# Flamingo block with routed experts on one core: biases loaded earlier, tile steps without a loop, table work cut in pieces, last gathers without a barrier

## The chip, the cores and the metric

One Trainium2 chip, one of its cores. The metric is the device time of one execution in microseconds (us). Four engines compute: PE (TensorE, matrix multiply, writes PSUM), DVE (VectorE), ACT (ScalarE) and POOL (GpSimd); SP (SyncE) only starts transfers. Each engine works through its own list of instructions and waits on semaphores for the others. PEld is the weight load of PE. A q behind an engine's name (DVEq, POOLq) is its sequencer, the part that reads the instructions, loads registers and waits.

## What is computed

```python
x = x + tanh(g_xattn) * attention(layernorm(x), ctx, ctx)     # 32 batches of 128 rows, width 512
z = layernorm(x)
logits = tanh(z @ Wg1.T) @ Wg2.T                              # 8 experts
top 2 experts of each row, weights = softmax of their two logits
up   = z @ Wup[e].T + bup[e]        # 512 -> 256
h    = silu(up)
down = h @ Wdown[e].T + bdown[e]    # 256 -> 512
x = x + tanh(g_ffn) * (weight1 * down1 + weight2 * down2)
```

All values are f32. The biases bup and bdown are the same for every row, so they are spread over all 128 partitions.

## The kernel before

**First phase.** A software pipeline of 39 steps does attention, norm and routing for 32 batches and scatters each normed row to two places in `slots`, one for each chosen expert. Batches 0 to 20 go to the first part, 21 to 31 to the second. At its end SP, PE, ACT and DVE meet at the semaphore `phase1_over`, and behind that SP loads the two biases (`bup` 1 MB, `bdn` 2 MB) and DVE, PE and ACT begin the tiles.

**Tiles.** The rows of `slots` are worked off in 78 tiles of 128 rows (49 of the first part, 29 of the second), each with one expert. In step s the engines work on several tiles at once: PE transposes the rows of tile s-1 (line 1096), transposes the activations of tile s-3 (L1103), multiplies tile s-2 by `Wup` (L1112 to 1114, 12 matmuls) and tile s-3 by `Wdown` (L1125 to 1127, 6 matmuls). Each f32 product is made of a high and a low part, so ACT copies the high part (`zh` L626, `hh` L621) and DVE makes the low part (`zl` L883, `hl` L877). DVE's order in a step is fixed by the code: read the expert's number from `tab_e` into a register (L295, a `TENSOR_LOAD` that its sequencer does), then `hl`, `zl`, `u_sb` (L892), `t_sb` (L896), `y_sb` (L905), then table work if the step has any, then the mixing of a batch. SP loads tile s and stores the result of tile s-4.

The steps 0 to 15 and 48 to 81 are written out; the steps 16 to 47 are a loop of two turns with 16 steps each (`tile_pipeline`).

**Tables.** `tables(part, n)` works out from the counts of each expert which expert and which rows a tile has (`tab_e`, `tab_r`) and where each row's result lies (`rows_all`). Each instruction reads what the one before wrote, so most go through `then`, which counts up `tab_step` and makes DVE wait for it. For the first part it runs in steps 30 to 34 of the first phase, and its last piece in tile step 5; the weights of the two choices (`coef`) follow in tile steps 6 and 7, and the second part's table in tile steps 8 to 12.

**Mixing.** From tile step 56 on, the 21 batches of the first part are finished beside the tiles: POOL gathers the two rows of each token from `expert_out` (L508), ACT and DVE scale, DVE and POOL add to `r_in`, SP stores. The 11 batches of the second part come after the last tile. Before that all five engines meet at `phase2_over`; then SP loads `r_late` (L400), POOL gathers (L527, 22 gathers), DVE adds twice for each batch and SP stores.

Of the kernel before, what the change touches and what calls it, by code (L numbers as in the profile page):

```python
# [23 lines left out]
P = 128  # L24
# [79 lines left out]
def block_kernel(nc, x_d, ctx_d, gx_d, gf_d, wg1_d, wg2_d, w_d, bup_d, bdn_d, out_d):  # L104
# [5 lines left out]
    with top:  # L110
# [41 lines left out]
        rows_f = sb("rows_f", [P, 2 * NA], F32, p12)  # L152
# [3 lines left out]

        z = [sb(f"z{i}", [P, D], F32, p1) for i in range(RING)]
        slot_i = [sb(f"slot_i{i}", [P, 2], I32, p1) for i in range(RING)]
# [5 lines left out]
        v_aug = [sb(f"v_aug{i}", [P, KV * 32], F32, p1) for i in range(RING)]  # L164
        q_t = [sb(f"q_t{i}", [P, D], F32, p1) for i in range(RING)]
        k_t = [sb(f"k_t{i}", [P, 2 * P], F32, p1) for i in range(RING)]
        probs = sb("probs", [P, KV * G * S], F32, p1)
# [39 lines left out]
        p23 = ExitStack()  # L207
        r_in = [sb(f"r_in{i}", [P, D], F32, p23) for i in range(RRING)]
# [7 lines left out]
        bup = sb("bup", [P, E * HE], F32, p2)  # L216
        bdn = sb("bdn", [P, E * D], F32, p2)             
# [53 lines left out]
        phase1_over, phase2_over = sem("phase1_over"), sem("phase2_over")  # L271
# [36 lines left out]
        def _(sp):  # L308
# [57 lines left out]
            def tile_step(s, u, fresh):  # L366
# [10 lines left out]
                if isinstance(s, int) and s >= 48 and s < 48 + RRING:  # L377
                    if s == 48:
                        sp.wait_ge(scatter_over, 1)
                    load_residual(s - 48)  # L380
# [784 lines left out]
```

## Time and profile before

| | |
|---|---|
| three timed runs | 813.27, 813.95, 819.04 us; median 813.95 |
| the profiled execution | 824.84 us, of which the span from first to last instruction is 823.1 |
| busy in the span | PE 689.5 us (84%), DVE 566.0 (69%), ACT 380.5 (46%), POOL 293.8 (36%) |
| mean granted TensorE clock | 0.946 of full speed |
| chain that ended last | PE 62%, DVE 15%, issue 8%, DMA 7%, POOL 4% |

A timeline row reads: start, length, engine, line, operation, output<-inputs, and in brackets how long the engine was idle before it and what ended that. "issue" is time in which an engine waited for nothing that the profile shows. Times count from the start of the span.

### The profile page before, as it was taken

The numbers are of one execution on the slowest core, as the hardware profiler recorded it, in microseconds if no ns is written. First come the engines' busy times: TensorE is split into PE (matmuls) and PEld (weight loads), VectorE is DVE, ScalarE is ACT, GpSimd is POOL, SyncE is SP. The second block draws the span as 40 slices with busy tenths as digits, with TensorE's granted clock in tenths as the row PEclk, the third lists the DMA queues.
The fourth block names the chain that finished last, engine by engine and source line by source line (L and its number), as shares of the span: only waits on it lengthen the run. The fifth ranks groups of instructions, "written<-read, shape, count | busy, mean of one in ns | idle before, by whom it ended". The sixth has DMA issues, their size and how long they took to land.

```text
span 823.1 us, 18197 instructions
## 1 busy us (share of the span) xinstructions
PE 689.5 (84%) x5232; PEld 465.5 (57%) x5233; DVE 566.0 (69%) x1543; ACT 380.5 (46%) x706; POOL 293.8 (36%) x406
## 2 busy tenths in 40 slices
PE   3788999999999999998897787999899978888700
PEld 2444554544444444454443676899789967767500
DVE  3567877877777777878863466777577757775625
ACT  2366766766666666666542232333233324433300
POOL 4123544545445454454333200000000026665465
PEclk9999999999999999999986699999999999999955
DMA  5532444434434344343222743444344659998778
GB/s 163 186 94 86 134 132 136 135 121 144 132 117 127 120 143 132 121 135 119 74 95 87 279 134 103 144 153 150 121 147 147 209 176 316 324 319 271 245 282 314
DMA packets 67845, 135.10 MB, mean 164 GB/s; under 512 B 8640, under 2 KB 12736, under 8 KB 67520
## 3 DMA queue, kind: packets, MB, share of 16 engines
q1 hardware_dynamic: 57088, 100.69, 38.1%
q0 software_dynamic: 10240, 33.56, 11.6%
q8 instruction: 33, 0.54, 0.3%
q14 instruction: 36, 0.29, 0.1%
q10 hardware_dynamic: 448, 0.02, 0.0%
HBM read 76.04 MB, written 58.20 MB: 163 GB/s over the span
## 4 chain that ended last, share of the span: by engine, by line
PE 62%; DVE 15%; issue 8%; DMA 7%; POOL 4%; SPq 2%; ACT 1%; DVEq 1%; another core or an unknown queue 1%; POOLq 0%; ACTq 0%
PE s_ps L979 11%; DVE nmax L762 9%; PE bank_a L958 7%; PE st_ps L1002 7%; PE bank_c L1019 3%; PE st_ps L1114 3%; PE st_ps L1112 3%; PE st_ps L1113 3%; PE s_ps L1096 3%; DMA z_s<-slots 3%; PE st_ps L1010 3%; POOL y_late L527 2%; PE bank_b L967 2%; DMA out<-r_in 2%; PE bank_c L1125 2%
## 5 line engine op out<-in xcount | busy, mean ns | idle before, releaser
L762 DVE TENSOR_REDUCE nmax<-s_ps 128x8 f32<-128x1024 f32 x128 | 156.4, 1222 | 91.0 <-PE s_ps L979 87.2
L979 PE MATMUL s_ps<-k_t,q_t 32*128 32x256 f32 x1024 | 153.8, 418 | 37.8 <-DVE nmax L762 35.8
L558 ACT ACTIVATE probs<-st_ps 128x1024 f32<-128x1024 f32 x128 | 131.1, 1024 | 115.5 <-PE st_ps L1010 113.0
L1002 PE MATMUL st_ps<-q_t,k_t 32*128 32x512 f32 x512 | 148.6, 656 | 1.2 <-ACT probs L558 1.0
L979 PEld LDWEIGHTS s_ps<-k_t,q_t 32*128 32x128 f32 x1024 | 91.9, 192 | 88.9 <-DVE nmax L762 49.2
L508 POOL DMA_INDIRECT y<-expert_out,rows_all x42 | 40.3, 960 | 205.9 <-DMA expert_out<-y_sb 196.3
L1112 PE MATMUL st_ps<-w_hi,zh 128*128 x312 | 96.5, 309 | 0.7 <-DVE zl L883 0.7
L1114 PE MATMUL st_ps<-w_hi,zl 128*128 x312 | 89.8, 288 | 0.0
L1113 PE MATMUL st_ps<-w_lo,zh 128*128 x312 | 89.3, 286 | 0.0
L631 ACT ACTIVATE t_sb<-u_sb 128x256 f32<-128x256 f32 x78 | 32.6, 417 | 109.7 <-DVE u_sb L892 105.3
L958 PE MATMUL bank_a<-probs,v_aug 128*32 128x512 f32 x512 | 70.8, 623 | 0.0
L485 POOL DMA_INDIRECT slots<-z,slot_i x64 | 64.4, 1006 | 16.4 <-issue 16.1
L1112 PEld LDWEIGHTS st_ps<-w_hi,zh 128*128 128x128 f32 x312 | 60.6, 194 | 1.1 <-issue 1.1
L1113 PEld LDWEIGHTS st_ps<-w_lo,zh 128*128 128x128 f32 x312 | 61.2, 196 | 0.0
L1096 PE MATMUL s_ps<-ident_f,z_s 128*128 128x128 f32 x312 | 49.2, 283 | 13.5 <-DMA z_s<-slots 11.8
L1114 PEld LDWEIGHTS st_ps<-w_hi,zl 128*128 128x128 f32 x312 | 60.3, 193 | 0.0
L896 DVE SCALAR_TENSOR_TENSOR t_sb<-t_sb,u_sb 128x256 f32<-128x256 f32 x78 | 33.2, 426 | 37.9 <-ACT t_sb L631 34.5
L883 DVE TENSOR_TENSOR zl<-s_ps,zh 128x512 fp32r<-128x512 f32 x78 | 53.7, 689 | 5.7 <-ACT zh L626 2.2
L1096 PEld LDWEIGHTS s_ps<-ident_f,z_s 128*128 128x128 f32 x312 | 38.8, 145 | 28.4 <-DMA z_s<-slots 16.2
L476 POOL TENSOR_TENSOR x_res<-x_res,z 128x512 f32<-128x512 f32 x32 | 40.5, 1267 | 30.3 <-DVE z L666 30.3
L1010 PE MATMUL st_ps<-nm_t,pick 32*128 32x512 bf16 x256 | 50.6, 382 | 0.0
L626 ACT ACTIVATE zh<-s_ps 128x512 fp32r<-128x512 f32 x78 | 46.3, 593 | 1.2 <-PE s_ps L1096 1.2
(153 smaller groups left out, 1423.7 us busy)
## 6 DMA issues: line engine op xcount, KB each, us to landing
z_s<-slots SPq DMA_DIRECT2D x78, 256.0 KB
expert_out<-y_sb SPq DMA_DIRECT2D x78, 256.0 KB
x_in<-in_x SPq DMA_DIRECT2D x32, 256.0 KB, 2.7
wst<-in_w SPq DMA_DIRECT2D x32, 256.0 KB, 2.6
x_res<-in_x SPq DMA_DIRECT2D x32, 256.0 KB
x_scratch<-x_res SPq DMA_DIRECT2D x32, 256.0 KB, 2.0
r_in<-x_scratch SPq DMA_DIRECT2D x21, 256.0 KB
out<-r_in SPq DMA_DIRECT2D x21, 256.0 KB
```

The lines of the kernel that those rows point to most:

```text
L485: g.indirect_dma_start(out=slots_d[int(split_at(b7))], out_offset=bass.IndirectOffsetOnAxis(ap=slot_i[q7][:, j:j + 1], axis=0), in_=z[q7][ ...
L558: a.activation(out, st_ps[:, :].rearrange("t (k n) -> t k n", k=2), ACT.Exp, scale=HD ** -0.5).then_inc(exp_done[half], 1)
L762: v.tensor_reduce(out, s_ps[:, :].rearrange("s (r g c t) -> s r g c t", r=2, g=2, c=2), X_AXIS, ALU.max, negate=True).then_inc(max_done, 1)
L883: v.tensor_tensor(zl[p][:, :], bank[p][:, :], zh[p][:, :].bitcast(F32), ALU.subtract).then_inc(zl_done, 1)
L958: last = t_.matmul(bank_a[32 * j:32 * j + 32, :], v_aug[r][:, 32 * k:32 * k + 32], probs[:, k * G * S:(k + 1) * G * S], start=True, stop=True,
L979: last = t_.matmul(s_ps[:, HALF * rr + 2 * P * gg:HALF * rr + 2 * P * (gg + 1)], q_t[r2][row:row + ROWS32, P * g_:P * (g_ + 1)], k_t[r2][r ...
L1002: t_.matmul(st_ps[:, HALF * rr:HALF * (rr + 1)], k_t[r][row:row + ROWS32, P * i:P * (i + 1)], q_t[r][row:row + ROWS32, :], start=True, sto ...
L1010: last = t_.matmul(st_ps[:, HALF * rr:HALF * (rr + 1)], pick[i][row:row + ROWS32, :], nm_t[p][row:row + ROWS32, :], start=False, stop=True ...
L1096: last = t_.transpose(bank[p][:, P * c:P * c + P], z_s[r][:, P * c:P * c + P], ident_f[:, :])
L1112: t_.matmul(o, zh[p][:, P * c:P * c + P], w_hi[:, cols], start=(c == 0), stop=False)
L1113: t_.matmul(o, zh[p][:, P * c:P * c + P], w_lo[:, cols], start=False, stop=False)
L1114: last = t_.matmul(o, zl[p][:, P * c:P * c + P], w_hi[:, cols], start=False, stop=(c == DC - 1))
```

## The change

Four things. (1) `bup` and `bdn` get memory that is free earlier, and SP loads them behind the loads of tiles 0 to 3 and ahead of `phase1_over`, after waits for the last readers of the memory. (2) `tile_pipeline` has no loop: all 82 steps are written out. The first four residual loads come in steps 40 to 43 instead of 48 to 51. (3) `tables` has 16 pieces instead of 5 (and one more for the first part): the first phase does three of them in each of steps 30 to 34, piece 15 of the first part is in tile step 6, the weights are in steps 8 to 11 (one instruction each), and the second part's pieces are in steps 14 to 29, one in each step. (4) `phase2_over` is gone: SP waits for the last matmul (`dn_done`) before it loads `r_late`, POOL for the last matmul and the last two stores of results (`y_stored`) before it gathers, DVE for its data.

```diff
 def tile_pipeline(eng, step):
-    first, last, unroll = 16, 48, 16
-    for s in range(first):
-        step(s, s % unroll, s == 0)
-    with eng.Fori(0, (last - first) // unroll) as i:
-        for u in range(unroll):
-            step(i * unroll + (first + u), u, u == 0)
-    for s in range(last, TILES + 4):
-        step(s, s % unroll, s == last)
+    for s in range(TILES + 4):
+        step(s, s % 16, s == 0)
...
             for t in range(RING):
                 load_tile(t, t)
+            sp.wait_ge(w_lo_done, B)
+            sp.wait_ge(n_done, B)
+            sp.wait_ge(kt_done, B)
+            sp.wait_ge(v_done, B)
+            sp.wait_ge(qt_done, B)
+            sp.wait_ge(st_done[1], 2 * B)
+            sp.wait_ge(pv_done, 2 * B)
+            sp.dma_start(bup[:, :], bup_d.to_broadcast([P, E * HE])).then_inc(bup_loaded, 16)
+            sp.dma_start(bdn[:, :], bdn_d.to_broadcast([P, E * D])).then_inc(bdn_loaded, 16)
             for p in range(2):
                 sp.wait_ge(res_stored[p], ring2(B - 2 + p, p))
             sp.drain().then_inc(phase1_over, 1)
             sp.wait_ge(phase1_over, 4)
-            sp.dma_start(bup[:, :], bup_d.to_broadcast([P, E * HE])).then_inc(bup_loaded, 16)
-            sp.dma_start(bdn[:, :], bdn_d.to_broadcast([P, E * D])).then_inc(bdn_loaded, 16)
...
             tile_pipeline(sp, tile_step)
-            for p in range(2):
-                last = TILES - 1 - (TILES - 1 - p) % 2
-                sp.wait_ge(y_stored[p], ring2(last, p))
-            sp.drain().then_inc(phase2_over, 1)
-            sp.wait_ge(phase2_over, 5)
+            sp.wait_ge(dn_done, TILES)
...
-            pool.drain().then_inc(phase2_over, 1)
-            pool.wait_ge(phase2_over, 5)
             pool.wait_ge(rows_done, 2)
+            pool.wait_ge(dn_done, TILES)
+            for p in range(2):
+                last = TILES - 1 - (TILES - 1 - p) % 2
+                pool.wait_ge(y_stored[p], ring2(last, p))
...
-                if isinstance(s, int) and 5 <= s < 8:
-                    tables(0, s)
-                if isinstance(s, int) and 8 <= s < 13:
-                    tables(1, s - 8)
+                if s == 6:
+                    tables(0, 15)
+                if 8 <= s < 12:
+                    weights_of_choices(s - 8)
+                if 14 <= s < 30:
+                    tables(1, s - 14)
```

On DVE, the first table step of the tiles (step 8 before): all instructions of `tables(1, 0)` stand between `y_sb` and the register load of the next step.

```order
L905 SCALAR_TENSOR_TENSOR y_sb<-bank_c,bdn 128x512
L692 TENSOR_TENSOR count<-run,ebase 128x8 [waits run_done]
L694 TENSOR_SCALAR upto<-e_diff 128x64 [waits tab_step]
L695 SCALAR_TENSOR_TENSOR past<-count,iota_t 128x88
L698 TENSOR_REDUCE ntile<-past 128x8 [waits tab_step]
L295 TENSOR_LOAD tab_e [waits tab_step]
L295 ISA x2
L877 TENSOR_TENSOR hl<-bank_q,hh 128x256 [waits dn_done,hh_done]
```

The same engine after the change, steps 14 and 15, which hold the first two of the sixteen pieces.

```order
L914 SCALAR_TENSOR_TENSOR y_sb<-bank_c,bdn 128x512
L693 TENSOR_TENSOR count<-run,ebase 128x8 [waits run_done]
L694 TENSOR_SCALAR upto<-e_diff 128x64
L288 TENSOR_LOAD tab_e [waits tab_step]
L288 ISA x2
L886 TENSOR_TENSOR hl<-bank_q,hh 128x256 [waits dn_done,hh_done]
L892 TENSOR_TENSOR zl<-s_ps,zh 128x512 [waits up_done,zh_done]
L901 ISA [waits tanh_done,up_done]
L901 TENSOR_TENSOR u_sb<-st_ps,bup 128x256
L905 SCALAR_TENSOR_TENSOR t_sb<-t_sb,u_sb 128x256 [waits ht_done,tanh_done]
L914 ISA [waits y_stored0,dn_done]
L914 SCALAR_TENSOR_TENSOR y_sb<-bank_b,bdn 128x512
```

The pieces are shorter, and the wait for `tab_step` still stands on the register load, now in each step that has a piece ending in `then`: 14 of the 16 table pieces and 3 of the 4 pieces of the weights.

On SP, the end of the tiles before:

```order
L376 DMA expert_out<-y_sb 128x512 [waits y_done]
L390 DMA out<-r_in 128x512 [waits mix2]
L400 DMA r_late<-x_scratch 128x512 [waits y_stored1,y_stored0,phase2_over]
L400 DMA r_late<-x_scratch 128x512 x10
L390 DMA out<-r_in 128x512 [waits mix2]
```

And after:

```order
L376 DMA expert_out<-y_sb 128x512 [waits y_done]
L390 DMA out<-r_in 128x512 [waits mix2]
L396 DMA r_late<-x_scratch 128x512 [waits dn_done]
L396 DMA r_late<-x_scratch 128x512 x10
L390 DMA out<-r_in 128x512 [waits mix2]
```

The places in the list are the same; the loads of `r_late` wait for the last matmul alone. On POOL the last gathers (L527) trade `phase2_over`, which stood behind POOL's own drain, for `dn_done` and `y_stored`.

## Rows read from the trace of the kernel before

**Rows 1.** Windows: start:end and length, busy time of PE, PEld, DVE, ACT, POOL, PE's clock, DMA.
```profile
586.00:655.80 69.80, 69.72 (x475) 62.73 (x474) 51.54 (x101) 25.39 (x59) 0.00 (x0) 1.00 0.52 164
655.80:780.00 124.20, 105.35 (x651) 88.50 (x649) 81.48 (x156) 47.78 (x102) 66.14 (x62) 0.97 0.84 277
784.00:786.40 2.40, 0.00 (x0) 0.00 (x0) 0.00 (x0) 0.00 (x0) 0.00 (x0) 0.50 0.00 0
```

**Rows 2.** Timeline of DVE, a step without table work.
```profile
516.95 0.69 DVE L905 SCALAR_TENSOR_TENSOR y_sb<-bank_c,bdn 128x512 f32<-128x512 f32 x1
517.91 0.42 DVE L877 TENSOR_TENSOR hl<-bank_q,hh 128x256 fp32r<-128x256 f32 x1 [0.27 <-ACT hh L621]
...
520.44 0.69 DVE L905 SCALAR_TENSOR_TENSOR y_sb<-bank_b,bdn 128x512 f32<-128x512 f32 x1
```

**Rows 3.** Timeline of DVE, tile steps 5 to 8 and the end of step 12.
```profile
476.48 0.69 DVE L905 SCALAR_TENSOR_TENSOR y_sb<-bank_b,bdn 128x512 f32<-128x512 f32 x1
...
477.44 0.42 DVE L877 TENSOR_TENSOR hl<-bank_a,hh 128x256 fp32r<-128x256 f32 x1 [0.18 <-ACT hh L621]
...
479.97 0.69 DVE L905 SCALAR_TENSOR_TENSOR y_sb<-bank_c,bdn 128x512 f32<-128x512 f32 x1
...
480.79 0.35 DVE L740 RECIPROCAL coef<-coef 128x32 f32<-128x32 f32 x1
481.88 0.42 DVE L877 TENSOR_TENSOR hl<-bank_q,hh 128x256 fp32r<-128x256 f32 x1 [0.74 <-DVE coef L740]
...
484.37 0.69 DVE L905 SCALAR_TENSOR_TENSOR y_sb<-bank_b,bdn 128x512 f32<-128x512 f32 x1 [0.23 <-PE bank_b L1127]
484.98 0.23 DVE L743 TENSOR_SCALAR coef<-coef,gates 128x32 f32<-128x32 f32 x1
...
485.96 0.42 DVE L877 TENSOR_TENSOR hl<-bank_a,hh 128x256 fp32r<-128x256 f32 x1 [0.52 <-issue]
...
488.43 0.69 DVE L905 SCALAR_TENSOR_TENSOR y_sb<-bank_c,bdn 128x512 f32<-128x512 f32 x1 [0.21 <-PE bank_c L1127]
...
490.88 0.42 DVE L877 TENSOR_TENSOR hl<-bank_q,hh 128x256 fp32r<-128x256 f32 x1 [1.01 <-DVE ntile L698]
...
513.46 0.69 DVE L905 SCALAR_TENSOR_TENSOR y_sb<-bank_b,bdn 128x512 f32<-128x512 f32 x1 [0.22 <-PE bank_b L1127]
```

**Rows 4.** Windows: sum over the five stretches that hold the second part's table work.
```profile
sum 5.44, PE 5.44 PEld 5.22 DVE 4.95 ACT 4.12 POOL 0.00; mean PE 1.09 PEld 1.04 DVE 0.99 ACT 0.82 POOL 0.00
```

**Rows 5.** Line 295: duration in ns min/median/max of DVE's register loads.
```profile
L295 DVEq TENSOR_LOAD <-tab_e x81: 298/305/673, 458.5 to 772.5; - x81
```

**Rows 6.** Timeline of DVE around the loop's begin and its second turn.
```profile
518.40 0.69 DVE L883 TENSOR_TENSOR zl<-s_ps,zh 128x512 fp32r<-128x512 f32 x1
...
533.16 0.69 DVE L883 TENSOR_TENSOR zl<-s_ps,zh 128x512 fp32r<-128x512 f32 x1
...
571.91 0.69 DVE L883 TENSOR_TENSOR zl<-s_ps,zh 128x512 fp32r<-128x512 f32 x1
...
581.81 0.42 DVE L877 TENSOR_TENSOR hl<-bank_a,hh 128x256 fp32r<-128x256 f32 x1 [3.56 <-issue]
...
593.79 0.69 DVE L883 TENSOR_TENSOR zl<-s_ps,zh 128x512 fp32r<-128x512 f32 x1
```

**Rows 7.** Timeline: SP's load of tile 3, and the first use of the bias.
```profile
451.87 0.34 SPq L349 DMA_DIRECT2D z_s<-slots  x1
...
461.78 0.41 PE L1114 MATMUL st_ps<-w_hi,zl 128*128 x1
...
462.77 0.42 DVE L892 TENSOR_TENSOR u_sb<-st_ps,bup 128x256 f32<-128x256 f32 x1 [2.69 <-DMA bup<-in_bup]
```

**Rows 8.** Chain that ended last (start, length, what), on POOL's queue behind its last addition.
```profile
782.87 3.59 issue
```

**Rows 9.** Waits of SP's queue from 775 to 790: us in total, times, longest.
```profile
SPq L396 <- DMA expert_out<-y_sb: 1.2, 1, 1.2
```

**Rows 10.** Timeline, the first late gather.
```profile
787.19 0.96 POOL L527 DMA_INDIRECT y_late<-expert_out,rows_all  x1 [4.32 <-POOLq L522]
```

More of the change, by code:

```diff
@@ L151, in block_kernel @@
         shift = sb("shift", [P, 2 * NA], F32, p12)
-        rows_f = sb("rows_f", [P, 2 * NA], F32, p12)
         p1 = ExitStack()
-        z = [sb(f"z{i}", [P, D], F32, p1) for i in range(RING)]
-        slot_i = [sb(f"slot_i{i}", [P, 2], I32, p1) for i in range(RING)]
         wst = sb("wst", [P, WCHUNK], F32, p1)
@@ L163, in block_kernel @@
         q_perm = sb("q_perm", [P, D], F32, p1)
-        v_aug = [sb(f"v_aug{i}", [P, KV * 32], F32, p1) for i in range(RING)]
         q_t = [sb(f"q_t{i}", [P, D], F32, p1) for i in range(RING)]
         k_t = [sb(f"k_t{i}", [P, 2 * P], F32, p1) for i in range(RING)]
+        v_aug = [sb(f"v_aug{i}", [P, KV * 32], F32, p1) for i in range(RING)]
+        z = [sb(f"z{i}", [P, D], F32, p1) for i in range(RING)]
+        slot_i = [sb(f"slot_i{i}", [P, 2], I32, p1) for i in range(RING)]
         probs = sb("probs", [P, KV * G * S], F32, p1)
@@ L207, in block_kernel @@
         p23 = ExitStack()
+        bup = sb("bup", [P, E * HE], F32, p23)
+        bdn = sb("bdn", [P, E * D], F32, p23)
         r_in = [sb(f"r_in{i}", [P, D], F32, p23) for i in range(RRING)]
@@ L215, in block_kernel @@
         p2 = ExitStack()
-        bup = sb("bup", [P, E * HE], F32, p2)
-        bdn = sb("bdn", [P, E * D], F32, p2)
         zh = [sb(f"zh{i}", [P, D], F32R, p2) for i in range(2)]
@@ L270, in block_kernel @@
         scattered = [sem(f"scattered{i}") for i in range(RING)]
-        phase1_over, phase2_over = sem("phase1_over"), sem("phase2_over")
+        phase1_over = sem("phase1_over")
         bup_loaded, bdn_loaded, scatter_over = sem("bup_loaded"), sem("bdn_loaded"), sem("scatter_over")
@@ L376, in tile_step @@
                     sp.dma_start(y_d[part][bass.ds((t - TILE0[part]) * P, P), :], y_sb[p][:, :]).then_inc(y_stored[p], 16)
-                if isinstance(s, int) and s >= 48 and s < 48 + RRING:
-                    if s == 48:
+                if isinstance(s, int) and s >= 40 and s < 40 + RRING:
+                    if s == 40:
                         sp.wait_ge(scatter_over, 1)
-                    load_residual(s - 48)
+                    load_residual(s - 40)
                 for m in mixed_at(s - 2 if isinstance(s, int) else s):
@@ L639, in _ @@
             tile_pipeline(act, tile_step)
-            act.drain().then_inc(phase2_over, 1)
         @block.vector
@@ L687, in tables @@
                 nt, t0 = NTILES[part], TILE0[part]
+                cols = slice(2 * first, 2 * (first + nb))
+                ov = past[:, 0:E * nb].rearrange("p (e i) -> p e i", e=E)
+                un = upton[:, :].rearrange("p (e i) -> p e i", e=E)
                 pv_ = past[:, 0:nt * E].rearrange("p (t e) -> p t e", e=E)
                 pw_ = pastw[:, 0:nt * E].rearrange("p (t e) -> p t e", e=E)
+                bv = pastw[:, 0:2 * nb * E].rearrange("p (n e) -> p n e", e=E)
                 if n == 0:
                     dve.wait_ge(run_done, first + nb)
-                    then(v.tensor_tensor(count[:, :], run[part][:, :], ebase[part][:, :], ALU.subtract))
-                    ov = past[:, 0:E * nb].rearrange("p (e i) -> p e i", e=E)
-                    step_of(v.tensor_scalar(upto[:, :], e_diff[:, :], 0.0, None, ALU.is_le))
+                    step_of(v.tensor_tensor(count[:, :], run[part][:, :], ebase[part][:, :], ALU.subtract))
+                    then(v.tensor_scalar(upto[:, :], e_diff[:, :], 0.0, None, ALU.is_le))
+                if n == 1:
                     then(v.scalar_tensor_tensor(ov, count[:, :].unsqueeze(2).to_broadcast([P, E, nb]), 1.0 / P,
@@ L697, in tables @@
                                                 ALU.mult, ALU.is_gt))
+                if n == 2:
                     then(v.tensor_reduce(ntile[:, :], ov, X_AXIS, ALU.add))
-                if n == 1:
-                    un = upton[:, :].rearrange("p (e i) -> p e i", e=E)
+                if n == 3:
                     step_of(v.memset(drop[:, E:E + 1], 0.0))
@@ L854, in step @@
                                     ALU.is_equal).then_inc(masks_done, 1)
-                if isinstance(s, int) and s >= TAB0 and s - TAB0 < 5:
-                    tables(0, s - TAB0)
+                if isinstance(s, int) and s >= TAB0:
+                    for n in range(3 * (s - TAB0), min(3 * (s - TAB0) + 3, 15)):
+                        tables(0, n)
             pipeline(dve, step, STEPS, LOOP0, NA + O_SLOT, RING)
@@ L919, in _ @@
             tile_pipeline(dve, tile_step)
-            dve.drain().then_inc(phase2_over, 1)
-            dve.wait_ge(phase2_over, 5)
             for i in range(NB):
@@ L1130, in _ @@
             tile_pipeline(pe, tile_step)
-            pe.drain().then_inc(phase2_over, 1)
 _INS = ["x", "ctx_512", "g_xattn", "g_ffn", "wg1", "wg2", "w", "bup", "bdn"]
```

35 lines of the change are left out of this document (20 added, 15 removed).

## The prediction

> **What bounds the kernel now.** I read the windows by stage first [rows 1]. From 586 to 655.8 us, tiles without any mixing, PE is busy 69.72 of 69.80 us: PE is the bound, and a step takes 3.50 us. From 655.8 to 780, beside the mixing, the DMA engines are busy 0.84 of the time and move 277 GB/s, and the 124 us are bought by transfers as much as by PE. From 784 to 786.4 no engine and no transfer does anything. So the reader should see three things to ask of each edit: does it stand in a PE-bound step, in the DMA-bound stretch (nothing here does), or in a pause.
>
> Then I read DVE's timeline step by step. In a step without table work `y_sb` starts at 516.95, `hl` at 517.91 and the next `y_sb` at 520.44 [rows 2]: 0.96 us and then 2.53 us, 3.49 together. The 2.53 us are a chain that leaves DVE and comes back: `hl`, the six matmuls with `Wdown`, `y_sb`. Where DVE is late this chain shrinks only to 2.47 us (485.96 to 488.43) [rows 3]. So a step stays at 3.50 us only while `hl` starts at most 3.50 - 2.47 = 1.03 us behind the start of `y_sb`, and each us beyond is paid in full. Though DVE is busy 69% of the span, what is put behind `y_sb` has only 1.03 - 0.96 = 0.07 us of cover. The 0.96 us hold one more thing: DVE's sequencer reads the expert's number during `y_sb`. A `then` in front of that read forbids it.
>
> **Part 3, the table in pieces.** Before, steps 6 to 12 hold this work. From 479.97 to 513.46 seven steps take 33.49 us [rows 3]; seven free ones take 24.5, so it costs 9.0 us.
>
> What does one piece cost? In step 7 one instruction with a wait behind it stands in the way (L743; L744 has no wait). `hl` starts 485.96 - 484.37 = 1.59 us behind `y_sb`, 0.56 too late. The instruction itself holds 0.25 of that, so 0.31 is fixed. In step 6 the two instructions run from about 480.58 to 481.14 (0.56), `hl` is at 481.88, 1.91 behind `y_sb` and 0.88 too late: fixed 0.32. In step 8 four instructions take 0.88 (one of the five stretches of [rows 4]), `hl` is at 490.88, 2.45 behind, 1.42 too late: fixed 0.54 [rows 3]. The fixed part is the register load with what follows it, which now starts only when the table instruction has ended. It took DVE 298 ns at the least, 305 in the median and 673 at the most [rows 5]. In step 5, where the one instruction has no wait, `hl` is 477.44 - 476.48 = 0.96 behind `y_sb`: free.
>
> After the change 14 table pieces and 3 of the weights end in a wait; the others are free like step 5. Their instructions: 5.44 us for the second part's [rows 4], less 0.52 for those at the ends of steps 11 and 12 that have no wait, so 4.9, and 0.56 + 0.25 for the weights: 5.7 together. With 17 times 0.32 it is 5.7 + 5.4 = 11.1 us. With 17 times 0.54 it is 14.9. Against 9.0 before, this edit loses **2.1 us** (up to 5.9). I take 0.32, since the short pieces come as early behind `y_sb` as those of steps 6 and 7 did. Cutting makes nothing cheaper: the sum of the instructions stays, and the fixed part is paid 17 times instead of 7. In the first phase the same instructions stay in the same steps 30 to 34, three pieces in each; nothing.
>
> The Trainium skill (DMA: Bandwidth & Descriptors, section Latency and other measured facts) gives a register load a floor of about 600 ns. The trace's median of 305 ns lies under it [rows 5]; by that floor each piece would cost 0.3 us more than I take, some 5 us in all, which is my second rival's case.
>
> **Part 2, no loop.** Loop turns cost time at two places. At the entry four steps from 518.40 to 533.16 take 14.76 us instead of 14.0: 0.8. At the second turn DVE starts `hl` at 581.81 after 3.56 us of "issue", and the five steps from 571.91 to 593.79 take 21.88 us instead of 17.5: 4.4 [rows 6]. "Issue" with all inputs there means that the sequencer has no instruction. Written out, both go: **5.2 us**. The steps that were written out before had no such stall, so I take nothing for the 32 new ones; they cost 0 to 2 us if the fetch is sometimes late. The residual loads eight steps earlier are four transfers in SP's queue in a stretch where the DMA engines are half idle (0.52) [rows 1]: nothing.
>
> **Part 1, biases early.** The first `u_sb` waits for `bup` until 462.77, while the last of its matmuls ends at 461.78 + 0.41 = 462.19 [rows 7]. SP issued the load of tile 3 at 451.87 [rows 7] and would issue `bup` right behind it instead of behind the barrier. `bup` then lands earlier by the same time, and half a us of it is enough: `u_sb` goes with the matmul, **0.5 us** (0 to 1). The seven new waits are on batches' work done before SP's last four tile loads; behind them in SP's list stand only its drain and `phase1_over`, for which DVE is the last. The 3 MB meet the last scatters, for which nobody waits until step 40. If SP's drain should hold until the biases have landed, the barrier opens late; I count that into the last rival.
>
> **Part 4, no barrier.** POOL's last addition ends at 782.87, then 3.59 us pass on POOL's queue in its drain, and only then the barrier opens [rows 8]; the last stores of results had landed at about 782.9, since SP waited 1.2 us for them behind its issue that ended at 781.7 [rows 9]. The first gather starts at 787.19 [rows 10]. Without drain and barrier it starts about 0.1 to 0.7 us behind 782.9, so 3.6 to 4.2 us earlier. What is late next is POOL's own issue of 22 gathers, 1.26 us each, which sets the tail before and after. The `r_late` loads start at 781.7 in the pause instead of together with the gathers, which can only relieve them. I take **3.8 us** (3 to 5).
>
> **Sum.** 0.5 + 5.2 + 3.8 - 2.1 = 7.4 us less. The profiled execution goes from 824.84 to 817.4. It was 10.9 us longer than the median of the three runs; I take the difference over unscaled: 813.95 - 7.4 = **806.5 us**.
>
> **Rivals.**
>
> *The pieces are dearer.* The fixed part is 0.54 for each, as in step 8. For it: steps 8 to 10 have it three times. Against: steps 6 and 7 have 0.32, and the new pieces are like those. Then 7.4 - 3.8 = 3.6 less: 810.3 us.
>
> *The pieces hide.* If the wait on `tab_step` costs nothing and the register load keeps its place under `y_sb`, a piece of 0.2 to 0.4 us fits into the gap in front of `hl` (0.27 us [rows 2]). Then the table costs about nothing instead of 9.0: 5.2 + 0.5 + 3.8 + 9.0 = 18.5 less, 795.5 us. For it: step 5 was free, and DVE is idle 31% of the time. Against: step 7, where one short instruction with a wait cost 0.56. The Trainium skill (VectorE: DVE Perf Modes, section The DRAIN you can't avoid) says that a semaphore behind each of a chain of DVE operations costs nothing extra; by that rule it would come out this way. The trace speaks against it where a register load, not another DVE operation, stands behind the wait.
>
> *The pause at the end stays.* The 3.6 us on POOL are not the drain but something the first late gather has to wait for in any case. For it: no row names what the drain waits for. Against: POOL's addition had ended, the stores had landed, and no transfer was under way [rows 1, 8, 9]. Then 7.4 - 3.8: 810.3 us, as the first.
>
> *Written-out steps starve.* Each of the 32 new step bodies is fetched for the first time, as the loop's first turn was, and two of the engines' lists grow. If a step lacks instructions for 0.24 us on the mean (7.4 / 32 = 0.23), the gain is gone; at 0.4 us it is 5 us slower, 819 us. For it: after a turn of the loop the sequencers stay behind for two more steps. Against: the steps written out before run at 3.50.
>
> **Chances.** My forecast 0.50; dearer pieces 0.18; hidden pieces 0.12; the pause stays 0.12; slower through fetch (or the drain on SP) 0.08. A measurement of this kernel tells about 1%, 8.1 us, from no change. Of my own case four in ten lie beyond that bound, 0.20, with the hidden pieces 0.32: faster 0.33, within 1% 0.60, slower 0.07. The range: the ends of the terms in my case are 0 + 3.5 + 3 - 5.9 = 0.6 and 1 + 5.2 + 5 - 2.1 = 9.1 less; the low end goes a little further towards the hidden pieces: 801.5 to 812.5.
>
> **What would show it.** In tile steps 14 to 29 of the new trace `hl` should start 1.5 to 1.9 us behind `y_sb` and a step should take 3.9 to 4.3 us, save in the steps of pieces 11 and 15. There should be no wait of 3 us for "issue" around tile 31. The first `u_sb` should wait for a matmul. The first late gather should start within a us of the last landed store, and the windows should show no stretch without transfers there. I am wrong if the register load slips under `y_sb` in spite of the wait, if the stall of the loop turns up elsewhere, or if the DMA-bound stretch of 124 us, which I leave as it is, comes out shorter or longer by some us.

## The result, and the profile after

The changed kernel takes 807.0 us in the median of 20 runs (802.6 to 817.9); before, on the same chip, takes 817.97 (20 runs). The ratio is 0.987, 95% interval 0.984 to 0.989: 10.7 us less (8.7 to 12.8). The forecast was 7.4 us less, 806.5 us. The profiled execution took 817.92 us, span 816.2, against 824.84 and 823.1 of before, so the two that can be compared row by row lie 6.9 us apart. Some executions are over 1.5% slower at a lower granted clock, the profiled ones of the changed kernel and of experiment 4 among them; the ratios here and below leave these out, the medians don't.

First the table step, on DVE's timeline of the changed kernel: the end of step 13, then the first two pieces, and far behind them a step without table work.

```profile
503.71 0.69 DVE L914 SCALAR_TENSOR_TENSOR y_sb<-bank_b,bdn 128x512 f32<-128x512 f32 x1
504.68 0.42 DVE L886 TENSOR_TENSOR hl<-bank_a,hh 128x256 fp32r<-128x256 f32 x1 [0.27 <-ACT hh L619]
...
507.17 0.69 DVE L914 SCALAR_TENSOR_TENSOR y_sb<-bank_c,bdn 128x512 f32<-128x512 f32 x1
...
507.85 0.18 DVE L694 TENSOR_SCALAR upto<-e_diff 128x64 f32<-128x64 f32 x1
508.78 0.42 DVE L886 TENSOR_TENSOR hl<-bank_q,hh 128x256 fp32r<-128x256 f32 x1 [0.74 <-ACT hh L619]
...
511.26 0.69 DVE L914 SCALAR_TENSOR_TENSOR y_sb<-bank_b,bdn 128x512 f32<-128x512 f32 x1 [0.22 <-PE bank_b L1136]
512.84 0.42 DVE L886 TENSOR_TENSOR hl<-bank_a,hh 128x256 fp32r<-128x256 f32 x1 [0.74 <-ACT hh L619]
...
515.32 0.69 DVE L914 SCALAR_TENSOR_TENSOR y_sb<-bank_c,bdn 128x512 f32<-128x512 f32 x1 [0.22 <-PE bank_c L1136]
...
589.41 0.69 DVE L914 SCALAR_TENSOR_TENSOR y_sb<-bank_b,bdn 128x512 f32<-128x512 f32 x1
590.37 0.42 DVE L886 TENSOR_TENSOR hl<-bank_a,hh 128x256 fp32r<-128x256 f32 x1 [0.27 <-ACT hh L619]
592.86 0.69 DVE L914 SCALAR_TENSOR_TENSOR y_sb<-bank_c,bdn 128x512 f32<-128x512 f32 x1
```

`hl` starts 1.61 and 1.58 us behind `y_sb` where a piece stands, 0.96 or 0.97 where none does; the steps take 4.09 and 4.06 us against 3.45. From `hl` to the next `y_sb` it takes 2.48 or 2.49 us with a piece and without; before had 2.47 and 2.53 [rows 2, 3]. The releaser named for a late `hl` is ACT's `hh`, but `hh` ended 0.93 us behind the start of `y_sb` in every one of these steps. Behind the piece, which ends at 508.03, DVE's sequencer runs the register load from 508.07 to 508.37 and what belongs to it until 508.66; in the free step ahead the load had started at 503.74, under `y_sb`. Experiments 1 and 2 test this reading. Without table work a step takes 3.45 or 3.46 us, not the 3.50 of before [rows 2]: nothing in the prediction has this.

The register load itself, by source line, in ns (minimum, median, maximum), answers to [rows 5]:

```profile
L288 DVEq TENSOR_LOAD <-tab_e x78: 299/304/1112, 456.7 to 769.1; - x78
```

The end of the tiles, on the timeline (POOL, SP and DVE), answers to [rows 8 to 10]:

```profile
776.40 0.69 DVE L914 SCALAR_TENSOR_TENSOR y_sb<-bank_c,bdn 128x512 f32<-128x512 f32 x1 [2.04 <-PE bank_c L1136]
777.12 0.32 SPq L376 DMA_DIRECT2D expert_out<-y_sb  x1
...
777.83 1.26 POOL L516 TENSOR_TENSOR r_in<-r_in,y 128x512 f32<-128x512 f32 x1 [2.45 <-DVE r_in L927]
...
779.99 0.96 POOL L525 DMA_INDIRECT y_late<-expert_out,rows_all  x1 [0.90 <-DMA expert_out<-y_sb]
```

The first late gather now waits for the landed store and nothing else. It starts 3.59 us behind the start of the last `y_sb` (7.01 us before, 780.18 to 787.19 [rows 10]).

Where the time went is read best between starts of `zl`, one for each tile. The n-th `zl` marks tile n-1. All numbers are us from DVE's timeline, and the last column runs to the end of the span.

| kernel | 2nd zl at | 2nd to 4th | 4th to 53rd | 53rd to 56th | 56th to 78th | 78th to end |
|---|---|---|---|---|---|---|
| before | 459.38 | 11.57 | 186.26 | 17.04 | 95.93 | 52.92 |
| after | 457.60 | 11.13 | 181.28 | 17.67 | 99.13 | 49.39 |
| difference | -1.78 | -0.44 | -4.98 | +0.63 | +3.20 | -3.53 |

The column from the 4th to the 53rd holds the loop, the table and the free steps; the last holds the barrier; the second holds the biases. The stretch from the 53rd to the 78th, in which the change has no term of the sum, is 3.8 us longer in this one execution; PE's mean granted clock in its two columns is 0.81 and 0.95 where before has 0.90 and 0.98.

### The profile page after: what moved, and what is told of

Its sections match the earlier page's. It is cut to its first block, busy times and chain, and to the rows that moved or that the text cites. A ratio compares the mean times of both kernels' runs of the same rounds, so it can differ in the third digit from the quotient of the medians.

```text
span 816.2 us, 17880 instructions
## 1 busy us (share of the span) xinstructions
PE 688.8 (84%) x5232; PEld 466.9 (57%) x5232; DVE 562.0 (69%) x1541; ACT 380.4 (47%) x706; POOL 293.8 (36%) x406
## 4 chain that ended last, share of the span: by engine, by line
PE 63%; DVE 15%; DMA 7%; issue 6%; POOL 3%; SPq 2%; DVEq 1%; ACT 1%; another core or an unknown queue 1%; PEld 0%; POOLq 0%; PEldq 0%
PE s_ps L988 12%; DVE nmax L770 9%; PE bank_a L967 8%; PE st_ps L1011 7%; DMA z_s<-slots 3%; PE bank_c L1028 3%; PE st_ps L1123 3%; PE bank_b L976 3%; PE st_ps L1121 3%; PE st_ps L1122 3%; DMA out<-r_in 3%; POOL y_late L525 3%; PE s_ps L1105 2%; PE st_ps L1019 2%; PE bank_c L1134 2%
```

## The experiments

All ratios below are against before on the same chip, with 95% intervals, and "the changed kernel" is the kernel of the result above. The first eight kernels ran on one chip, where before has a median of 808.2 to 808.3 us, the next two on a second (before 807.96), the last two on a third (before 819.22). The same table for all twelve comes behind them.

**1. The wait for a piece moved to the front of the next piece.** The changed kernel; a piece's last instruction counts up `tab_step` as before, but DVE waits for it only where the next piece begins, one tile step later.

```diff
+            def settle():
+                if link[0]:
+                    dve.wait_ge(tab_step, link[0])
...
+                last = then if part == 0 else step_of
+                if part == 1:
+                    settle()
...
                 if n == 2:
-                    then(v.tensor_reduce(ntile[:, :], ov, X_AXIS, ALU.add))
+                    last(v.tensor_reduce(ntile[:, :], ov, X_AXIS, ALU.add))
```

> The changed kernel, but a piece of the second part's table or of the weights no longer waits for its own end: the wait for tab_step stands in front of the next piece's instruction, one step later. If the price of a piece is the register load that starts only behind the wait, hl starts 0.96 to 1.1 us behind y_sb (1.5 to 1.8 in the changed kernel) in all of these steps except the one with two dependent instructions, the 11.4 us that the pieces cost shrink to 0.5 to 1.5, and the kernel is 10 us faster than the changed one, some 797 us where that has 807. If the instructions themselves or the semaphore cost the time, the steps stay at 3.9 to 4.3 us and nothing changes.

Measured: 783.87 us, ratio 0.968 (0.964 to 0.973). DVE's timeline of this kernel, two steps with one instruction each and then the piece with two dependent ones:

```profile
500.76 0.69 DVE L924 SCALAR_TENSOR_TENSOR y_sb<-bank_b,bdn 128x512 f32<-128x512 f32 x1
501.37 0.24 DVE L705 SCALAR_TENSOR_TENSOR past<-count,iota_t 128x88 f32<-128x88 f32 x1
501.73 0.42 DVE L896 TENSOR_TENSOR hl<-bank_a,hh 128x256 fp32r<-128x256 f32 x1
504.21 0.69 DVE L924 SCALAR_TENSOR_TENSOR y_sb<-bank_c,bdn 128x512 f32<-128x512 f32 x1
504.82 0.23 DVE L709 TENSOR_REDUCE ntile<-past 128x8 f32<-128x88 f32 x1
505.17 0.42 DVE L896 TENSOR_TENSOR hl<-bank_q,hh 128x256 fp32r<-128x256 f32 x1
...
511.31 0.69 DVE L924 SCALAR_TENSOR_TENSOR y_sb<-bank_c,bdn 128x512 f32<-128x512 f32 x1 [0.20 <-PE bank_c L1146]
512.87 0.42 DVE L896 TENSOR_TENSOR hl<-bank_q,hh 128x256 fp32r<-128x256 f32 x1 [0.55 <-issue]
```

The same instructions at the same places, and `hl` is 0.97 and 0.96 us behind `y_sb` instead of 1.58. An instruction of 0.24 us fits under the 0.27 us that DVE is idle there anyway [rows 2]. Only the piece with a wait left inside it is late (1.56). From the 8th to the 30th `zl` this kernel takes 76.91 us where the changed one takes 87.47: with 22 free steps of 3.455 (76.0) the table costs 0.9 us here and 11.5 there. So it is the wait's place that costs; experiment 2 tells the wait from the load behind it.

**2. The register load moved ahead of the piece, the wait left where it was.**

```diff
+                if 8 <= s < 11 or 14 <= s < 30:
+                    ahead.append(expert_of(dve, s - 1))
                 if s == 6:
                     tables(0, 15)
...
-                    expert[0] = expert_of(dve, s - 2)
+                    expert[0] = ahead.pop() if ahead else expert_of(dve, s - 2)
```

> The changed kernel, with the same waits behind each piece, but the expert's number of the next step is read into its register in front of the piece instead of behind it. If it is the order of wait and register load that costs, hl starts about 1.0 us behind y_sb for short pieces and 1.1 to 1.3 for those of 0.4 us and more, and 9 to 10 us of the 11.4 go. If a wait of DVE for its own instruction costs 0.3 us by itself, wherever the load stands, at most 2 us go.

Measured: 792.61 us, ratio 0.982 (0.976 to 0.988). DVE's timeline at the piece of one instruction that the changed kernel has at 511.87, after its `y_sb` of 511.26:

```profile
495.31 0.69 DVE L914 SCALAR_TENSOR_TENSOR y_sb<-bank_b,bdn 128x512 f32<-128x512 f32 x1
495.96 0.25 DVE L696 SCALAR_TENSOR_TENSOR past<-count,iota_t 128x88 f32<-128x88 f32 x1
496.32 0.42 DVE L886 TENSOR_TENSOR hl<-bank_a,hh 128x256 fp32r<-128x256 f32 x1
```

The stretch from the 8th to the 30th `zl` is 77.89 us, so the table costs 1.9; `hl` is 1.01 to 1.18 us behind `y_sb` in most pieces, though DVE waits behind each piece as in the changed kernel. The wait itself is nearly free: what cost 0.32 us was that the load could not start before it. Two different edits, which both let the load go ahead of the wait, take 10.6 and 9.6 us off this stretch; with that the price of a piece is shown. The medians of the two lie 8.7 us apart, which the steps do not explain; the four runs of experiment 2 spread from 785.8 to 796.5 us.

**3. The changed kernel with the old table.** `tables`, its calls and `rows_f` as in before, the rest as after.

```diff
-                if s == 6:
-                    tables(0, 15)
-                if 8 <= s < 12:
-                    weights_of_choices(s - 8)
-                if 14 <= s < 30:
-                    tables(1, s - 14)
+                if 5 <= s < 8:
+                    tables(0, s)
+                if 8 <= s < 13:
+                    tables(1, s - 8)
```

> The changed kernel with the table and the weights in the pieces and steps of the kernel before (steps 5 to 12, seven steps with waits). By the sum of the prediction the stretch costs 9.0 us instead of 11.4, so this is 2 to 2.5 us faster than the changed kernel, too little for the times but to be read from the steps. If cutting had helped, it would be slower than the changed kernel.

Measured: 798.18 us, ratio 0.988 (0.983 to 0.993). The table costs 8.9 us (from the 6th to the 14th `zl` 36.93 us, less eight steps of 3.50), against 11.5 in sixteen pieces. But from the 4th to the 53rd `zl` it takes 180.52 us and not 2.6 less than the changed kernel's 181.28, since its free steps take 3.50 us again. The two prices are each counted from the kernel's own free step (3.455 and 3.50), so their difference is not what the cut costs; experiments 3 and 5 together give that, below. That raised the question of experiments 5 and 6.

**4. POOL's drain put back alone** in front of the last gathers, with no meeting of the engines.

```diff
+            pool.drain().then_inc(pool_quiet, 1)
+            pool.wait_ge(pool_quiet, 1)
             pool.wait_ge(rows_done, 2)
```

> The changed kernel, and POOL drains its pipe once behind its last addition, with no barrier and no other engine in it. If the 3.6 us in front of the last gathers were POOL's own drain, the first late gather again starts 7 us behind the last y_sb instead of 3.6, and the kernel is 3.4 us longer than the changed one. If they were the meeting of five engines, the drain costs under 0.5 us and nothing changes.

Measured: 800.9 us, ratio 0.991 (0.987 to 0.994). POOL's and DVE's timeline at the end of the tiles:

```profile
766.54 0.69 DVE L916 SCALAR_TENSOR_TENSOR y_sb<-bank_c,bdn 128x512 f32<-128x512 f32 x1 [3.47 <-PE bank_c L1138]
...
767.97 1.26 POOL L516 TENSOR_TENSOR r_in<-r_in,y 128x512 f32<-128x512 f32 x1 [3.89 <-DVE r_in L929]
773.65 0.96 POOL L527 DMA_INDIRECT y_late<-expert_out,rows_all  x1 [4.42 <-POOLq L518]
```

7.11 us from `y_sb` to the gather, as before had 7.01, though only POOL waits here, and only for itself. The drain on POOL's queue (duration in ns, start in us):

```profile
L518 POOLq DRAIN  x1: 4807/4807/4807, 767.9 to 767.9; - x1
```

It begins with POOL's last addition and ends 3.51 us behind the end of it. The trace of before has a drain of the same 4807 ns. POOL's own drain is the pause; what the drain waits for no run shows.

**5 and 6. The addresses.** One is the changed kernel with an unused tensor of 168 bytes per partition where `rows_f` was; the other is before without `rows_f`, its values kept in `shift`.

```diff
 (changed kernel)
         shift = sb("shift", [P, 2 * NA], F32, p12)
+        pad = sb("pad", [P, 2 * NA], F32, p12)
 (before)
-        rows_f = sb("rows_f", [P, 2 * NA], F32, p12)
...
-    step_of(v.tensor_tensor(rows_f[:, cols], slot_all[:, cols], shift[:, 0:2 * nb], ALU.subtract))
+    step_of(v.tensor_tensor(shift[:, cols], slot_all[:, cols], shift[:, 0:2 * nb], ALU.subtract))
...
-    v.tensor_copy(rows_all[:, 0:2 * NA], rows_f[:, 0:2 * NA]).then_inc(rows_done, 1)
+    v.tensor_copy(rows_all[:, 0:2 * NA], shift[:, 0:2 * NA]).then_inc(rows_done, 1)
```

> This is the changed kernel with one more tensor that nothing uses: 168 bytes per partition at the place in memory where before had rows_f, so that every tensor behind it gets the address that it had before, apart from the biases. Theory A (addresses): the removed rows_f moved all later tensors by 168 bytes, and that is why a tile step without table work takes 3.46 us in the changed kernel and in three experiments, and 3.50 in before and in the experiment with the old table. Then the step is 3.50 here again, and the time between the zl of tile steps 2 and 53 is about 2.2 us longer than in the changed kernel (183.5 for 181.3). Theory B (instructions): the step is shorter because DVE's instructions or their order differ; then it stays at 3.46 and the stretch at 181.3.

> The kernel before without rows_f: the first part's rows are worked out in the tensor shift, in place, so that all later tensors lie 168 bytes lower; nothing else differs. Theory A (addresses): a tile step without table work goes from 3.50 to 3.46 us, and 49 of them give 2.2 us, of a time of some 808 (ratio about 0.997). Theory B (instructions): the step stays at 3.50, ratio 1.000.

Measured: 801.94 us (ratio 0.988, 0.971 to 1.004) and 808.78 us (1.001, 0.996 to 1.006): the medians can't show two us. The steps can. First DVE's timeline of the changed kernel with the unused tensor, three starts of `y_sb`:

```profile
601.13 0.69 DVE L915 SCALAR_TENSOR_TENSOR y_sb<-bank_c,bdn 128x512 f32<-128x512 f32 x1
604.62 0.69 DVE L915 SCALAR_TENSOR_TENSOR y_sb<-bank_b,bdn 128x512 f32<-128x512 f32 x1
608.11 0.69 DVE L915 SCALAR_TENSOR_TENSOR y_sb<-bank_c,bdn 128x512 f32<-128x512 f32 x1
```

3.49 us a step, while the same instructions without the tensor take 3.45 or 3.46. In before without `rows_f` (experiment 6) the steps between the 36th and the 39th `zl` take 3.46, 3.46 and 3.45 us where before has 3.50. PE's groups of both kernels between 585 and 640 us (line, tiles, count, busy us, mean ns of one); the changed kernel with the tensor, then without, the latter from 585.1:

```profile
L1122 PE MATMUL st_ps<-w_hi,zh 128*128 x63 | 19.1, 303 | 0.0
L1124 PE MATMUL st_ps<-w_hi,zl 128*128 x62 | 17.5, 283 | 0.0
L1123 PE MATMUL st_ps<-w_lo,zh 128*128 x62 | 17.4, 280 | 0.0
```

```profile
L1121 PE MATMUL st_ps<-w_hi,zh 128*128 x64 | 19.3, 301 | 0.0
L1122 PE MATMUL st_ps<-w_lo,zh 128*128 x64 | 17.9, 280 | 0.0
L1123 PE MATMUL st_ps<-w_hi,zl 128*128 x64 | 17.9, 279 | 0.0
```

The matmuls of `w_hi` with `zl` take 283 ns instead of 279 and those of `w_hi` with `zh` 303 instead of 301; those of `w_lo` take 280 in both. Theory A holds in both directions, but its price was wrong: 1.4 us from the 4th to the 53rd `zl` (182.26 against 180.8 to 180.9 in four kernels without the tensor; 186.26 against 184.78), not 2.2. I had counted all 49 steps, and in a step with table work DVE, not PE, sets the length (4.09 us in the first piece at either address).

Experiments 5 and 3 have the old addresses both, and differ in the table: 182.26 us from the 4th to the 53rd `zl` with sixteen pieces, 180.52 with the old five. The cut costs 1.7 us.

**7. Before with the tile steps written out** and nothing else (the first hunk of the diff).

> The kernel before with the tile steps written out and nothing else. My sum gave this 5.2 us: 0.8 at the loop's begin and 4.4 at its second turn; the ratio would be 0.9936, the steps at both places 3.50 like their neighbours, and no other step longer. A rival: the written-out steps starve an engine elsewhere, and single steps between 16 and 53 show stalls of 0.3 us or more that sum to more than 1 us; the ratio is then above 0.996.

Measured: 800.49 us, ratio 0.993 (0.988 to 0.998). From the 4th to the 53rd `zl` 180.64 us, 5.6 less than before. DVE's timeline where before had its 3.56 us of "issue" [rows 6]:

```profile
572.73 0.69 DVE L877 TENSOR_TENSOR zl<-s_ps,zh 128x512 fp32r<-128x512 f32 x1
576.24 0.69 DVE L877 TENSOR_TENSOR zl<-s_ps,zh 128x512 fp32r<-128x512 f32 x1
579.81 0.69 DVE L877 TENSOR_TENSOR zl<-s_ps,zh 128x512 fp32r<-128x512 f32 x1
583.31 0.69 DVE L877 TENSOR_TENSOR zl<-s_ps,zh 128x512 fp32r<-128x512 f32 x1
```

3.51, 3.57 and 3.50 us; no step between the 14th and the 53rd `zl` takes more than 3.58. Nothing starves.

**8. The changed kernel with the biases loaded behind `phase1_over`,** in their new memory.

```diff
-            sp.wait_ge(w_lo_done, B)
...
-            sp.wait_ge(pv_done, 2 * B)
-            sp.dma_start(bup[:, :], bup_d.to_broadcast([P, E * HE])).then_inc(bup_loaded, 16)
-            sp.dma_start(bdn[:, :], bdn_d.to_broadcast([P, E * D])).then_inc(bdn_loaded, 16)
             for p in range(2):
                 sp.wait_ge(res_stored[p], ring2(B - 2 + p, p))
             sp.drain().then_inc(phase1_over, 1)
             sp.wait_ge(phase1_over, 4)
+            sp.dma_start(bup[:, :], bup_d.to_broadcast([P, E * HE])).then_inc(bup_loaded, 16)
+            sp.dma_start(bdn[:, :], bdn_d.to_broadcast([P, E * D])).then_inc(bdn_loaded, 16)
```

> The changed kernel with the loads of both biases back behind phase1_over, their memory as in the changed kernel. My sum gave the early loads 0.5 us: the first u_sb waits for the bias again, 2.7 us idle on DVE ahead of it for under 2 without, and from the second to the fourth zl it is 11.6 us instead of 11.1; ratio to the changed kernel 1.0006, which its time can't show. A rival by which the early loads are worth 1.8 us or more: the end of the first phase is later as well, since SP issued the biases in front of its waits for the stores; then the first tile step starts 1 us or more later than in the changed kernel, beyond what it varies between runs.

Measured: 798.05 us, ratio 0.989 (0.978 to 0.999). The second `zl` starts at 451.30 us, within the 443.7 to 452.5 of the other experiments, so there is no sign of the rival; a spread of 9 us would hide its 1.8, though. The first `u_sb` goes with its matmul (2.34 us idle on DVE, released by PE), and the first `y_sb` waits 1.01 us for `bdn`; 9.76 us pass from the 2nd to the 4th `zl`, 0.3 to 0.5 more than in the four kernels that have 9.26 to 9.42 with early loads. The size was right and the place was not: here it is `bdn` that is late, and not `bup`.

**9. The best version.** Experiment 1, and the piece with two dependent instructions split.

```diff
                 if n == 4:
-                    then(v.tensor_reduce(tend[:, :], un, X_AXIS, ALU.add))
+                    last(v.tensor_reduce(tend[:, :], un, X_AXIS, ALU.add))
+                if n == 4.5 or (part == 0 and n == 4):
                     last(v.scalar_tensor_tensor(row0[:, :], tend[:, :], float(-P), run[part][:, :], ALU.mult, ALU.add))
...
-                if 14 <= s < 30:
-                    tables(1, s - 14)
+                if 14 <= s < 31:
+                    tables(1, s - 14 if s < 19 else 4.5 if s == 19 else s - 15)
```

> The changed kernel with the wait for a piece's result moved to the front of the next piece, one tile step later, and the one piece whose second instruction reads the first split in two, so the table has 17 pieces in steps 14 to 30. If the price of a piece is the wait ahead of the register load, no step holds more than about 0.1 us over its neighbours: the experiment with the wait moved alone had 0.9 us over in the table stretch, 0.57 of it in the piece that is now split, so about 0.4 stays, and the time is 0.3 to 0.6 us under that experiment's, which this measurement can't tell; against before some 0.97. A rival: each further piece has a fixed price of its own whatever it waits for, and the stretch is not shorter than before the split.

Measured: 789.58 us, ratio 0.969 (0.964 to 0.975). No table step has `hl` more than 1.00 us behind `y_sb` (1.14 in the second step of the weights), and from the 4th to the 53rd `zl` it takes 169.77 us, 0.5 less than experiment 1. On time alone the two can't be told apart; both beat the changed kernel.

**10. The meeting of all five engines put back.** The changed kernel with `phase2_over` as in before.

> The changed kernel with the meeting of all five engines in front of the last gathers put back as in before. The experiment with POOL's drain alone had 7.11 us from the last y_sb to the first late gather, as before had 7.01 and the changed kernel 3.59. If the drain is the whole price, this one has 7.0 to 7.2 as well. If the meeting adds a hop of its own it has 7.3 or more. Time against the changed kernel: 3.5 us more.

Measured: 799.24 us, ratio 0.989 (0.985 to 0.993). DVE's and POOL's timeline:

```profile
752.49 0.69 DVE L917 SCALAR_TENSOR_TENSOR y_sb<-bank_c,bdn 128x512 f32<-128x512 f32 x1 [2.06 <-PE bank_c L1142]
...
754.17 1.26 POOL L520 TENSOR_TENSOR r_in<-r_in,y 128x512 f32<-128x512 f32 x1 [2.72 <-DVE r_in L930]
759.74 0.96 POOL L527 DMA_INDIRECT y_late<-expert_out,rows_all  x1 [4.31 <-POOLq L522]
```

7.25 us, 0.14 more than with the drain alone, and POOL's drain again has 4807 ns: the meeting adds next to nothing to it.

**11 and 12. The residual loads.** The changed kernel with the first four residual loads back in steps 48 to 51, and experiment 7 with them in steps 40 to 43.

```diff
-                if isinstance(s, int) and s >= 40 and s < 40 + RRING:
-                    if s == 40:
+                if isinstance(s, int) and s >= 48 and s < 48 + RRING:
+                    if s == 48:
                         sp.wait_ge(scatter_over, 1)
-                    load_residual(s - 40)
+                    load_residual(s - 48)
```

> The changed kernel with the first four residual loads back in steps 48 to 51, the one part of the change that my sum put at nothing and no run has tried alone. Theory C: the loads matter, since the first gathers of the mixing follow them at step 53. The three traces with loads at 48 have 12.8, 13.1 and 17.0 us from the 53rd to the 56th zl, and nine with loads at 40 have 10.4 to 10.7 in five, 11.3 to 12.4 in three and 17.7 in the changed kernel's own; then this run has 12.8 or more, and the time is some 2.4 us above the changed kernel's. Theory D: the loads have landed long before the first gathers (the last is issued 6 us ahead of them), and the spread of these four steps is chance, how the loads of tiles meet the gathers; then it has anything from 10.4 to 17, and the time doesn't move.

> The kernel before with the tile steps written out and the first four residual loads in steps 40 to 43, to stand beside the experiment that had the steps written out alone (13.1 us from the 53rd to the 56th zl). Theory C (the loads matter): 10.4 to 10.7 us there, and the ratio to before is 0.990 instead of 0.993. Theory D (chance): anything from 10.4 to 17 there, ratio 0.993.

Measured: 807.59 us (0.984, 0.979 to 0.990) and 812.68 us (0.992, 0.988 to 0.996), no difference to the changed kernel (0.987) and to experiment 7 (0.993) that the intervals tell. From the 53rd to the 56th `zl` they take 16.93 us (late loads) and 17.84 (early loads), so theory C falls: the early loads have the longer stretch. But theory D as I put it, chance, is not what the table shows either:

| experiment | 2nd zl at | 2nd to 4th | 4th to 53rd | 53rd to 56th | 56th to 78th | 78th to end |
|---|---|---|---|---|---|---|
| 1 wait deferred | 451.36 | 9.26 | 170.24 | 12.44 | 93.82 | 50.08 |
| 2 load hoisted | 443.67 | 11.06 | 171.37 | 11.31 | 96.64 | 50.05 |
| 3 old table | 446.16 | 10.98 | 180.52 | 10.59 | 95.06 | 50.69 |
| 4 drain | 451.64 | 10.92 | 180.94 | 12.12 | 99.89 | 54.49 |
| 5 unused tensor | 451.45 | 10.86 | 182.26 | 10.64 | 97.15 | 48.54 |
| 6 before, no rows_f | 450.25 | 11.12 | 184.78 | 12.80 | 97.33 | 52.32 |
| 7 before, no loop | 451.18 | 11.05 | 180.64 | 13.13 | 97.15 | 52.75 |
| 8 biases late | 451.30 | 9.76 | 180.92 | 10.72 | 93.78 | 49.92 |
| 9 best | 447.57 | 9.42 | 169.77 | 10.62 | 100.48 | 49.94 |
| 10 meeting back | 445.86 | 9.26 | 180.91 | 10.37 | 96.47 | 52.83 |
| 11 residuals late | 452.50 | 9.27 | 180.83 | 16.93 | 95.98 | 49.19 |
| 12 no loop, early | 451.15 | 11.05 | 180.50 | 17.84 | 95.58 | 53.48 |

The four traces with 17 us or nearly there are before, after and the last two; the changed kernel and the last two ran where before takes 818 to 819 us (the first profile came with runs of 813 to 819). The ten others, on two chips where before takes 808, have 10.4 to 13.1. ACT's timeline in experiment 11:

```profile
644.18 0.42 ACT L629 ACTIVATE t_sb<-u_sb 128x256 f32<-128x256 f32 x1 [1.61 <-issue]
650.15 0.38 ACT L619 ACTIVATE hh<-bank_a 128x256 fp32r<-128x256 f32 x1 [5.55 <-remote]
```

and in the changed kernel:

```profile
651.96 0.42 ACT L629 ACTIVATE t_sb<-u_sb 128x256 f32<-128x256 f32 x1 [1.99 <-DVE u_sb L901]
657.16 0.38 ACT L619 ACTIVATE hh<-bank_a 128x256 fp32r<-128x256 f32 x1 [4.78 <-remote]
```

PE had written `bank_a` by 645.55 in experiment 11, and ACT took it 4.6 us later, while POOL issued the first gathers of the mixing. PE then stands idle for 4.29 us, and its mean granted clock over the three steps is 0.90 (0.81 to 0.90 in the four traces, 1.00 in nine of the others and 0.91 in experiment 7). The profile names only something outside its records. What holds ACT there on the slower chip and not on the others was not tried.

## Why the prediction was right, and where it was not

The time, 807.0, is half a us from the forecast and inside its range; the direction and the mechanism of each part held. That it came out to half a us is luck: the three runs that it started from have a median 4 us below that of the 20 that came with the result, and the gain was forecast 3.3 us too small (7.4 for 10.7). The two errors cancel. The chances leaned to "within 1%" (0.60), and the ratio of 0.987 is a gain of 1.3%. The range is narrower than the sum behind it: 0.6 us less would be 813.4, not 812.5, and with 2 us for late fetches, as the text has it, the low end of the gain is 0.3 and not 0.6. Step by step:

- *Table in pieces, +2.1.* Measured +1.7, with the addresses equal (experiments 5 and 3). `hl` stood 1.52 to 1.82 us behind `y_sb` where 1.5 to 1.9 was forecast, and a step took 4.0 to 4.3 (forecast 3.9 to 4.3). The fixed part of 0.32 us holds, the 0.54 of the rival doesn't. Nor does the further price of 0.3 us more for each piece, some 5 us; it would be the case of the first rival (dearer pieces), not of the second, as the prediction has it. Experiments 1 and 2 show what the fixed part consists of.
- *No loop, -5.2.* Measured -5.6 by the steps and 0.993 by the ratio in experiment 7. The rival of starving steps is refuted.
- *Biases, -0.5.* Measured -0.44 in the two profiles and 0.3 to 0.5 in experiment 8. Right in size.
- *No barrier, -3.8.* Measured -3.4 from `y_sb` to the first gather, -3.5 to the end of the span. The rival that the pause stays is refuted, and experiment 4 pins the pause on POOL's drain.
- *The table in its old place would be better:* the sum said so (2.1 us), and experiments 3 and 5 show 1.7. This can't be seen in the medians, and the changed kernel wins most of it back by its addresses: 181.28 us from the 4th to the 53rd `zl`, and 180.8 to 180.9 in four kernels like it, against 180.52 in experiment 3.
- *The step that failed: the sum took a free step as 3.50 us on both sides.* It is 3.455 in the changed kernel, worth 1.4 us, because a tensor of 168 bytes went away. The full diff shows that line, and I read it as bookkeeping.
- *"The DMA-bound stretch I leave as it is."* It holds no gain of the change that a run shows, but it spreads by more than any term: 93.8 to 100.5 us from the 56th to the 78th `zl`.

The terms as measured sum to 0.4 + 5.6 + 3.5 - 1.7 + 1.4 = 9.2 us. The two profiles say the same without the terms: 0.44 + 4.98 + 3.53 = 8.95 us in the three columns that hold the terms. The ratio says 10.7 (8.7 to 12.8), so the sum lies inside the interval, and no further term is needed. For experiment 1 it is not enough: 25.8 us (22.2 to 29.3) stand against 9.2 + 10.6 = 19.8, and what brings the other 6.0 (2.4 to 9.5) stays open. Two places could hold it and neither was tried alone. The second `zl` comes at 450.25 to 459.38 in the four kernels with the old memory of the first phase and at 443.67 to 457.60 in the ten with the new order of `z`, `slot_i` and `v_aug`; the ranges overlap. And the clock, below, rises earlier in some of the kernels with the new memory.

## What to carry to other kernels

Where PE sets the length of a step and a chain through DVE is nearly as long, work put into that chain has as much cover as the chain is shorter than the step: here 0.07 us, though DVE was idle 31% of the time. Before cutting serial work into pieces, look at what stands behind each piece's wait: a wait in front of a register load cost 0.32 us each time plus the piece, and moving that wait to where the next piece begins, or the load ahead of it, made the same pieces nearly free (11.5 us to 0.9 or 1.9). Where a tensor is added or removed, compare a free step before and after, since the addresses of all later ones move (0.045 us a step here). And count two costs from the same base: the table's 11.5 and 9.0 us are each true against their own kernel's free step, and their difference is 0.8 us more than the cut costs.

## What the runs showed of the hardware

- **Addresses.** 168 bytes of shift in the tensors behind `rows_f` change a PE-bound step between 3.455 and 3.50 us (matmuls of `w_hi` with `zl` 279 and 283 ns), in both directions and in two kernels. Which tensor's address matters was not tried.
- **A drain on POOL.** It took 4807 ns each time, in before and in experiments 4 and 10, and ended 3.5 us behind POOL's last addition, whether four other engines met there or none. The first gather starts 4.3 to 4.4 us behind that addition with the drain and 0.90 without.
- **The clock after the first phase.** In the first tile steps PE's granted clock is 0.50, the 1.2 GHz level, and rises to 1.00 (2.4 GHz) at different times. Windows of the changed kernel from the 2nd `zl` on (start:end and length, busy time of PE, PEld, DVE, ACT, POOL, PE's clock, DMA share, GB/s), and then of experiment 11:

```profile
457.60:461.60 4.00, 3.67 (x16) 3.27 (x16) 1.17 (x3) 0.42 (x1) 0.20 (x1) 0.50 0.98 414
461.60:465.60 4.00, 3.57 (x16) 3.48 (x17) 1.66 (x4) 0.87 (x2) 0.00 (x0) 0.50 0.88 355
465.60:468.73 3.13, 3.13 (x22) 2.82 (x21) 1.80 (x4) 1.29 (x3) 0.00 (x0) 0.91 0.00 0
```

```profile
452.50:456.50 4.00, 3.66 (x16) 3.26 (x16) 1.18 (x3) 0.42 (x1) 0.18 (x1) 0.50 0.96 408
456.50:460.50 4.00, 3.58 (x25) 3.27 (x26) 2.37 (x6) 1.29 (x3) 0.00 (x0) 0.95 0.92 365
```

The same instructions take 11.13 us there and 9.27 here. The traces fall into two groups, 10.9 to 11.6 and 9.3 to 9.8; none of the four with the old memory and late biases is in the shorter one, and of the ten with the new memory five are and five are not. Whether the change helps to get there, the runs don't settle.

- **The same kernel took 808 us on two chips and 819 on a third.** Of these some 10 us, 4 to 7 lie in three steps at the begin of the mixing, where ACT stands still for 5 us. That the chip is the cause is inferred from four traces of one kind and ten of the other.
